# Quantising the next input tile in three steps of the chunk loop instead of two

## The chip, the cores and the metric

The kernel runs on one core of a Trainium2 chip. The metric is the device time of one execution in microseconds (us); the time before is 1630.95 us, the median of three runs. In the profile, PE is TensorE, PEld its weight loads, DVE is VectorE, ACT is ScalarE, POOL is GpSimd and SP is SyncE, whose queue starts the transfers.

## What is computed

A decoder layer with three blocks for 8 batches of 512 rows of 512 values. Only the last block is touched by the change. Its input and its inner result are rounded in blocks of 32 values with a common power of two as scale; the sum of the three parts is the output.

```
x = x + dilated_self_attention(layernorm(x))
x = x + cross_attention(layernorm(x), ctx_512, Wq, Wkv_expand, Wout)
x = x + ffn(layernorm(x), w_gate, w_up, w_down)

def ffn(x):                                   # weights quantised too
    inter = silu(q_act(x) @ w_gate.T) * (q_act(x) @ w_up.T)
    return q_act(inter) @ w_down.T

def q_act(x):                                 # blocks of 32 along the last axis
    sexp  = floor(log2(max|x| of the block)) - 2
    q     = round_to_small_float(x / 2**sexp) # 2 exponent, 3 mantissa bits, at most 7.5
    return q * 2**sexp
```

## The kernel before

Until about 178 us the weights of the last block are quantised and turned, and the self attention of batch 0 runs. Then each of the 8 batches goes through the same two stages. The first is cross attention (some 82 us, lines 871 to 886 and their counterparts on the other engines). The second is the chunk loop, which the change touches: `for i in range(P1_STEPS)`, with steps 0 to 20, of which 0 to 15 bring a chunk of the last block. Tile t of a batch (128 rows, four tiles) has the chunks 4t to 4t+3 (512 of the 2048 inner columns each). Beside these chunks run, in the same loop, the self attention and the head of the cross attention of the next batch; the last batch (b = 7) has none of that beside it.

Every engine has its own list, written out by hand in program order, and they meet through semaphores alone. What one step of the loop holds:

- TensorE: at i % 4 == 0 `turn_xq(t)` turns the quantised input tile `xq` into PSUM (line 1168) and `keep_busy` adds four products that nothing reads (L1060). Then `gate_up(i)` (L1181) makes gate and up of the chunk. It needs the slot that `gated(i - 2)` sets free, since the slots A and B alternate. Then come `down(i - 4)` (L1203) and `turn_inter(i - 3)` (L1192), and then the pieces of the next batch's attention: the turn L639, the scores L647, the value product L529 and the output L657, one after another over the four steps of a tile.
- ScalarE: `take_xq` copies the turned tile (L988), `silus(i)` (L995), `take_inter(i - 3)` (L1003), and for the next batch a copy, the exponential of the scores (L619, with a table load before it and one after it, ahead of the next silu) and a copy.
- VectorE: `gated(i)` multiplies up by silu (L838), takes block maxima (L812), their exponents (L815), the scales (L845) and their reciprocals (L846). `round_inter(i - 1)` clips and rounds into `q8` (L808). Then come `take_down` at steps 7, 11, 15 (L855), statistics (L498 to L500), and for the next batch the sums and divisions (L576, L578, L585), `normalise` (L511) and `shift2_of` (L516).
- GpSimd: `scale_inter(i)` and `scale_back(i - 1)` multiply by scales (both recorded at L696: `inter<-inter,rscale` and `iq<-q,scale`), `power` makes a reciprocal root (L506), `attend_pool` adds (L544), and `scale_x` and `scale_back_x` do for the next input tile what the first two do for a chunk (L696: `x_f<-x_f,rscale` and `xq<-q,scale`).

The next input tile t+1 is quantised during tile t. At step 4t, `quantise_x(t + 1)` on VectorE does normalisation into `x_f` (L511), maxima (L812), exponents (L815), scales (L827) and reciprocals (L828). GpSimd's `scale_x(t + 1)` stands at the end of step 4t. At step 4t+1, `round_x(t + 1)` on VectorE (L808, `q<-x_f`) is followed by GpSimd's `scale_back_x(t + 1)` at the end of the step. `turn_xq(t + 1)` on TensorE needs it at step 4t+4. For tile 0 this is done ahead of the loop.

Of the kernel before, what the change touches and what calls it, by code (L numbers as in the profile page):

```python
# [45 lines left out]
RING = 4  # L46
# [60 lines left out]
def decoder_layer(nc, x, ctx_t, wq_t, wkv_t, wo_t, w_gate, w_up, w_down, out):  # L107
# [3 lines left out]
    T = N // P  # L111
# [15 lines left out]
    with es:  # L127
# [92 lines left out]
        def until_filled(eng, label):  # L220
            s, k = slot_of[label]
            eng.wait_ge(filled[s], k + 1)
# [63 lines left out]
        with nc.Block() as block:  # L286
            @block.sync
            def _(sp):
                for j in range(RAW):
                    load_weights(sp, j)  # L290
                sp.dma_start(wq_raw[:], wq_t.rearrange("(c p) n -> p c n", p=P)).then_inc(wq_loaded, 16)
                sp.dma_start(wkv_raw[:], wkv_t).then_inc(wkv_loaded, 16)
                sp.dma_start(wo_sb[:], wo_t.rearrange("(c p) n -> p c n", p=P)).then_inc(wo_loaded, 16)
                for j in range(STEPS - RAW):

                    sp.wait_ge(wy_ready, j + 1)
                    load_weights(sp, j + RAW)
                sp.wait_ge(wo_loaded, 16)
# [204 lines left out]
        def power(pool, p, t):  # L503
            k = (p - 1) * T + t % T
            pool.wait_ge(S[f"var{p}_ready"], t + 1)
            pool.tensor_tensor(rstd[:, k:k + 1], var_eps[:, k:k + 1], minus_half[:],  # L506
                               ALU.pow).then_inc(S[f"rstd{p}_ready"], 1)

        def normalise(dve, dst, src, p, t):
            k = (p - 1) * T + t % T  # L510
            return dve.tensor_scalar(dst, src, moments[:, k, 0:1], rstd[:, k:k + 1], ALU.subtract, ALU.mult)  # L511
# [157 lines left out]
        with nc.Block() as block:  # L669
# [22 lines left out]
            @block.gpsimd  # L692
            def _(pool):

                def by_scales(dst, src, scales, signal):
                    pool.tensor_tensor(dst.rearrange("p (n k) -> p n k", k=BLOCK),  # L696
                                       src.rearrange("p (n k) -> p n k", k=BLOCK),
                                       scales.unsqueeze(2).to_broadcast([P, CH // BLOCK, BLOCK]),
                                       ALU.mult).then_inc(S[signal], 1)

                def scale_x(t):
                    pool.wait_ge(S["scale_x"], t + 1)
                    by_scales(x_f[:], x_f[:], rscale[:, RING, :], "x_scaled")

                def scale_back_x(t):
                    pool.wait_ge(S["q8x_ready"], t + 1)
                    if t >= 2:
                        until_filled(pool, ("xqT", t - 2))
                    by_scales(xq[:, t % 2, :], q8[:, RING + t % 2, :], scale6[:, RING + t % 2, :], "xq_ready")

                def scale_inter(i):
                    pool.wait_ge(S["scales_ready"], i + 1)
                    by_scales(inter[:, i % RING, :], inter[:, i % RING, :], rscale[:, i % RING, :],
                              "scaled_ready")

                def scale_back(i):
                    pool.wait_ge(S["q8_ready"], i + 1)
                    if i >= RING:
                        until_filled(pool, ("interT", i - RING))
                    by_scales(iq[:, i % RING, :], q8[:, i % RING, :], scale6[:, i % RING, :], "iq_ready")  # L720

                for i in range(P1_STEPS):
                    attend_pool(pool, 0, i)
                for b in range(B):
                    last = b + 1 == B
                    power(pool, 3, b * T)
                    scale_x(b * T)
                    power(pool, 3, b * T + 1)
                    scale_back_x(b * T)
                    if not last:  # L730
                        attend_pool(pool, b + 1, 0)
                    for i in range(P1_STEPS):
                        if i < CHUNKS:
                            scale_inter(b * CHUNKS + i)
                        if 1 <= i <= CHUNKS:
                            scale_back(b * CHUNKS + i - 1)
                        if i in STATS_AT:
                            power(pool, 3, b * T + STATS_AT[i])
                        if i and not last:
                            attend_pool(pool, b + 1, i)  # L740
                        if i % 4 == 0 and i // 4 + 1 < T:
                            scale_x(b * T + i // 4 + 1)
                        if i % 4 == 1 and i // 4 + 1 < T:
                            scale_back_x(b * T + i // 4 + 1)

            @block.vector
            def _(dve):
# [62 lines left out]
                def powers_of(src, r):  # L810

                    link(dve.tensor_reduce(top[:, r, :], in_blocks(src), AX_X, ALU.max,  # L812
                                           apply_absolute_value=True))
                    bits = top[:, r, :].bitcast(I32)
                    link(dve.tensor_scalar(bits, bits, EXPONENT, None, ALU.bitwise_and))  # L815

                def quantise_x(t):
                    r = RING + t % 2
                    dve.wait_ge(S["rstd3_ready"], t + 1)
                    if t:  # L820
                        dve.wait_ge(S["q8x_ready"], t)
                    link(normalise(dve, x_f[:], x_res[:, t % T, :], 3, t))
                    powers_of(x_f[:], RING)
                    if t >= 2:

                        dve.wait_ge(S["xq_ready"], t - 1)
                    link(dve.tensor_scalar(scale6[:, r, :], top[:, RING, :], TINY, ACT_SHIFT, ALU.max, ALU.mult))  # L827
                    dve.reciprocal(rscale[:, RING, :], scale6[:, r, :]).then_inc(S["scale_x"], 1)  # L828

                def round_x(t):  # L830
                    dve.wait_ge(S["x_scaled"], t + 1)
                    clip(q8[:, RING + t % 2, :], x_f[:]).then_inc(S["q8x_ready"], 1)
# [37 lines left out]
                for b in range(B):  # L870

                    first, end = b * UNITS, (b + 1) * UNITS
                    for pr in range(2):
                        maxima(first, pr)
                    for u in range(first, end):
                        oc, qt = units[u]
                        more = oc % OC + 1 < OC
                        if u + 1 < end:
                            maxima(u + 1, 0)
                        take_probs(u, 0)  # L880
                        recips(u)
                        if place[qt] == 0 and oc % OC:
                            take_out(oc - 1)
                        if u + 1 < end:
                            maxima(u + 1, 1)
                        take_probs(u, 1)
                    take_out((b + 1) * OC - 1)

                    last = b + 1 == B
                    take_y(b * T)  # L890
                    moments3(b * T)
                    take_y(b * T + 1)
                    quantise_x(b * T)
                    take_y(b * T + 2)
                    moments3(b * T + 1)
                    round_x(b * T)
                    if not last:
                        attend_vector(dve, link, b + 1, 0)
                    take_y(b * T + 3)
                    if not last:  # L900
                        attend_vector(dve, link, b + 1, 1)
                    for i in range(P1_STEPS):
                        if i < CHUNKS:
                            gated(b * CHUNKS + i)
                        if i % 4 == 3 and i > 4:
                            take_down(b * T + i // 4 - 1)
                        if 1 <= i <= CHUNKS:
                            round_inter(b * CHUNKS + i - 1)
                        if i in STATS_AT:
                            moments3(b * T + STATS_AT[i])  # L910
                        if i >= 2 and not last:
                            attend_vector(dve, link, b + 1, i)
                            head(b + 1, i)
                        if i % 4 == 0 and i // 4 + 1 < T:
                            quantise_x(b * T + i // 4 + 1)
                        if i % 4 == 1 and i // 4 + 1 < T:
                            round_x(b * T + i // 4 + 1)

            @block.scalar
# [378 lines left out]
```

## Time and profile before

| | us |
|---|---|
| median of 3 runs | 1630.95 (1624.5 to 1632.29) |
| profiled execution, its own time | 1628.43 |
| span of the profile | 1626.6 |
| busy: TensorE, VectorE, ScalarE, GpSimd | 1372.0, 1152.6, 859.4, 546.8 |
| chunk loop of batch 1, first gate product to last silu product | 468.8 to 537.7 |
| chunk loop of batch 7, first gate product to last addition | 1557.7 to 1623.3 |

The busy time over the whole span hides that the stages have different limits, so the rows below are taken from the chunk loops. Batch 1 stands for the batches 0 to 6: the 16 gate products (L838) of a chunk loop stand at the same distances from one another in all seven, within 0.1 us. In a timeline row, the first number is the start of the instruction, the second its duration. What is in brackets at the end is how long the engine stood idle before it and who ended that. The profile can show an instruction as started while it is still held back; its duration is then longer than that of its like.

### The profile page before, as it was taken

The page shows a single profiled execution, that of the slowest core. Times are in us where ns is not written, and L with a number is a line of the kernel's source. Part 1 is how long each engine was busy: PE and PEld are TensorE (multiplying, and loading weights), DVE is VectorE, ACT ScalarE, POOL GpSimd, SP SyncE. Part 2 cuts the span into 40 slices and gives each one's busy share as a digit, 9 for nine tenths or more (in the row PEclk, how much of TensorE's full clock was granted, in tenths as well). Part 3 has the DMA queues.
Part 4 walks back from the last instruction along what each step waited for, and adds up shares of the span by engine and source line. Part 5 has one row for each costly group of instructions (what it writes and reads, how often), then busy time and mean ns, then how long its engine had stood idle before and what let it go on. Part 6 is the DMA issues. An engine that isn't in the chain of part 4 may idle for free.

```text
span 1626.6 us, 31184 instructions
## 1 busy us (share of the span) xinstructions
PE 1372.0 (84%) x11267; PEld 792.3 (49%) x11344; DVE 1152.6 (71%) x2475; ACT 859.4 (53%) x2098; POOL 546.8 (34%) x494
## 2 busy tenths in 40 slices
PE   0223999889998899889998999889988899889987
PEld 0112665445544565445544564455544564455533
DVE  8995555885569656985679555985579556975577
ACT  2542564556635664556635564556635664556622
POOL 5883100660037201660047201660047201750055
PEclk9999999999999999999999999999999999999999
DMA  6321000000010000000010000000010000000001
GB/s 199 98 78 39 1 2 14 21 14 15 2 27 15 20 1 15 21 14 14 2 27 14 21 1 17 18 19 9 2 27 14 21 2 27 8 21 2 2 0 26
DMA packets 25285, 36.07 MB, mean 22 GB/s; under 512 B 2480, under 2 KB 10672, under 8 KB 25136
## 3 DMA queue, kind: packets, MB, share of 16 engines
q1 hardware_dynamic: 25136, 34.09, 7.8%
q8 instruction: 93, 1.52, 0.4%
q14 instruction: 56, 0.46, 0.1%
HBM read 25.69 MB, written 8.39 MB: 21 GB/s over the span
## 4 chain that ended last, share of the span: by engine, by line
PE 43%; DVE 32%; ACT 7%; issue 6%; POOL 3%; DMA 0%; SPq 0%; ACTq 0%; POOLq 0%; DVEq 0%
PE psum L1103 9%; PE psum L1120 9%; PE psum L529 8%; DVE top L812 6%; PE psum L1141 5%; DVE inter L838 4%; PE psum L1157 4%; DVE q L808 3%; PE psum L1106 3%; ACT p L957 3%; DVE nmx L762 2%; DVE top L815 2%; DVE stats L498 2%; DVE x_f L511 2%; DVE tmp L585 1%
## 5 line engine op out<-in xcount | busy, mean ns | idle before, releaser
L762 DVE TENSOR_REDUCE nmx<-psum 128x2 f32<-128x1024 f32 (+3 forms) x256 | 210.7, 823 | 167.0 <-PE psum L1106 166.3
L506 POOL TENSOR_TENSOR rstd<-var_eps,minus_half 128x1 f32<-128x1 f32 x96 | 58.2, 610 | 794.2 <-DVE var_eps L500 793.9
L957 ACT ACTIVATE p<-psum,nmx 128x384 f32<-128x384 f32 (+3 forms) x512 | 265.8, 527 | 64.0 <-DVE nmx L762 42.9
L775 DVE COPY pt<-psum 128x512 f32<-128x512 f32 (+3 forms) x256 | 124.7, 487 | 129.1 <-PE psum L1120 127.5
L1120 PE MATMUL psum<-ident,p 128*128 128x128 f32 x1280 | 204.8, 281 | 12.5 <-ACT pt L981 6.9
L1103 PE MATMUL psum<-k_f,q_f 32*128 32x512 f32 (+3 forms) x1024 | 206.9, 480 | 5.8 <-ACT p L957 5.3
L696 POOL TENSOR_TENSOR inter<-inter,rscale 128x512 f32<-128x512 f32 x128 | 140.1, 1095 | 143.7 <-DVE rscale L846 134.1
L1203 PE MATMUL psum<-wd_sb,iq_t 128*128 128x512 bf16 x483 | 135.3, 394 | 35.9 <-DVE x_res L855 29.3
L1120 PEld LDWEIGHTS psum<-ident,p 128*128 128x128 f32 x1280 | 138.6, 140 | 53.4 <-issue 19.0
L981 ACT COPY pt<-psum 128x512 f32<-128x512 f32 (+3 forms) x256 | 109.2, 426 | 97.8 <-PE psum L1120 95.5
L1181 PE MATMUL psum<-wg_sb,xq_t 128*128 128x512 bf16 x504 | 134.7, 391 | 20.3 <-DVE inter L838 20.3
L995 ACT ACTIVATE silu<-psum 128x512 f32<-128x512 f32 x128 | 76.4, 597 | 142.4 <-PE psum L1181 142.2
L696 POOL TENSOR_TENSOR iq<-q,scale 128x512 bf16<-128x512 fp8e4 x128 | 143.7, 1123 | 8.7 <-DVE q L808 8.7
L1003 ACT COPY iq_t<-psum 128x512 bf16<-128x512 bf16 x128 | 74.9, 585 | 123.9 <-PE psum L1192 123.9
L1181 PE MATMUL psum<-wu_sb,xq_t 128*128 128x512 bf16 x510 | 136.2, 391 | 0.1
L1157 PE MATMUL psum<-wo_sb,xn 128*128 128x512 f32 x256 | 118.0, 610 | 6.5 <-DVE xn L790 6.5
L428 PE MATMUL psum<-ident_b,w_q 128*128 128x128 bf16 x192 | 26.3, 309 | 112.7 <-POOL w_q L335 108.7
L1103 PEld LDWEIGHTS psum<-k_f,q_f 32*128 32x128 f32 x1024 | 76.9, 183 | 61.7 <-issue 43.2
L838 DVE TENSOR_TENSOR inter<-psum,silu 128x512 f32<-128x512 f32 x128 | 86.2, 674 | 24.6 <-ACT silu L995 23.9
L957 ACT ACTIVATION_READ_ACCUMULATOR p<-psum,nmx 128x1 f32 x512 | 103.0, 201 | 0.0
L529 PE MATMUL psum<-x_t,wq_hl 128*128 128x512 f32 (+1 forms) x480 | 100.1, 358 | 0.3
L1141 PE MATMUL psum<-pt,v_sb 128*32 128x128 f32 x2560 | 96.4, 277 | 3.2
(104 smaller groups left out, 2372.3 us busy)
## 6 DMA issues: line engine op xcount, KB each, us to landing
x_in<-in_x_dram SPq DMA_DIRECT2D x32, 256.0 KB, 4.0
out_dram<-x_res SPq DMA_DIRECT2D x64, 128.0 KB, 2.4
w_raw<-in_w_gate_dram SPq DMA_DIRECT2D x16, 256.0 KB, 2.8
w_raw<-in_w_up_dram SPq DMA_DIRECT2D x16, 256.0 KB, 3.1
w_raw<-in_w_down_dram SPq DMA_DIRECT2D x16, 256.0 KB, 3.9
ctx_in<-in_ctx_t_dram SPq DMA_DIRECT2D x8, 256.0 KB, 2.8
wq_raw<-in_wq_t_dram SPq DMA_DIRECT2D x1, 1024.0 KB, 8.4
wo_sb<-in_wo_t_dram SPq DMA_DIRECT2D x1, 1024.0 KB, 10.1
```

The lines of the kernel that those rows point to most:

```text
L529: last = pe.matmul(dst, w, x, start=(n == 0), stop=(stop and n == len(terms) - 1))
L696: pool.tensor_tensor(dst.rearrange("p (n k) -> p n k", k=BLOCK), src.rearrange("p (n k) -> p n k", k=BLOCK), scales.unsqueeze(2).to_broadc ...
L762: dve.tensor_reduce(nmx2[:, u % UNITS, 2 * pr:2 * pr + 2], where(("scores2", oc, qt, pr))[:, :, 0:(qt + 1) * P], AX_X, ALU.max, negate=Tru ...
L775: free(dve.tensor_copy(pt2[:, hh, 0:m], where(label)[:, 0, 0:m]), label)
L838: free(dve.tensor_tensor(inter[:, r, :], where(label)[:, 1, :], silu[:, i % 2, :], ALU.mult), label)
L957: ins = act.activation(p2[:, (4 * u + hh) % P2_RING, 0:m], where(label)[:, hh % 2, 0:m], ACT.Exp, bias=nmx2[:, u % UNITS, hh:hh + 1], accu ...
L1103: pe.matmul(where(label)[:, j, 0:m], q_f[rows, oc % 2, qt * P:(qt + 1) * P], k_f[rows, oc % 2, 0:m], start=True, stop=False)
L1120: last = pe.transpose(where(label)[:, 0, kt * P:(kt + 1) * P], p2[:, (4 * u + hh) % P2_RING, kt * P:(kt + 1) * P], ident[:])
L1141: last = pe.matmul(where(("outT", oc))[rows, 0, qt * P:(qt + 1) * P], v_sb[:, kt, h * HD:(h + 1) * HD], pt2[:, hh, kt * P:(kt + 1) * P], s ...
L1157: last = pe.matmul(where(label)[:, 0, :], out_n[:, oc, t % T * P:(t % T + 1) * P], wo_sb[:, oc, :], start=(oc == 0), stop=(oc == OC - 1))
L1181: last = pe.matmul(where(label)[:, j, :], xq_t[:, t % 2, c * P:(c + 1) * P], w[:, c, m * CH:(m + 1) * CH], start=(c == 0), stop=(c == C - 1))
L1203: last = pe.matmul(where(label)[:, 0, :], iq_t[:, i % RING, j * P:(j + 1) * P], wd_sb[:, 4 * m + j, :], start=(m == 0 and j == 0), stop=(m ...
```

## The change

`quantise_x` is split into `normalise3` and `scales_x`. Ahead of the loop the two are called one after the other, as before. In the loop, VectorE does `normalise3` at i % 4 == 0, `scales_x` at i % 4 == 1 (was 0) and `round_x` at i % 4 == 2 (was 1). GpSimd's `scale_x` stands at i % 4 == 1 (was 0) and `scale_back_x` at i % 4 == 2 (was 1), both at the end of the step. TensorE, ScalarE and SyncE keep their lists. No instruction is added or removed. In the changed kernel the lines behind `normalise3` have numbers two higher (L838 is L840 there), and those of TensorE's part five higher.

```diff
@@ GpSimd, chunk loop
-                        if i % 4 == 0 and i // 4 + 1 < T:
+                        if i % 4 == 1 and i // 4 + 1 < T:
                             scale_x(b * T + i // 4 + 1)
-                        if i % 4 == 1 and i // 4 + 1 < T:
+                        if i % 4 == 2 and i // 4 + 1 < T:
                             scale_back_x(b * T + i // 4 + 1)
@@ VectorE
-                def quantise_x(t):
-                    r = RING + t % 2
+                def normalise3(t):
                     dve.wait_ge(S["rstd3_ready"], t + 1)
                     if t:
                         dve.wait_ge(S["q8x_ready"], t)
                     link(normalise(dve, x_f[:], x_res[:, t % T, :], 3, t))
+
+                def scales_x(t):
+                    r = RING + t % 2
                     powers_of(x_f[:], RING)
...
@@ VectorE, chunk loop
                         if i % 4 == 0 and i // 4 + 1 < T:
-                            quantise_x(b * T + i // 4 + 1)
+                            normalise3(b * T + i // 4 + 1)
                         if i % 4 == 1 and i // 4 + 1 < T:
+                            scales_x(b * T + i // 4 + 1)
+                        if i % 4 == 2 and i // 4 + 1 < T:
                             round_x(b * T + i // 4 + 1)
```

VectorE's list from the end of step 4 to the start of step 6 of the first batch's chunk loop, before:

```order
347 L511 TENSOR_SCALAR x_f<-x_res,moments,rstd 128x512
348 L812 TENSOR_REDUCE top<-x_f 128x16
349 L815 TENSOR_SCALAR top<-top 128x16
350 L827 TENSOR_SCALAR scale<-top 128x16
351 L828 RECIPROCAL rscale<-scale 128x16
352 L838 TENSOR_TENSOR inter<-psum,silu 128x512
...
357 L808 TENSOR_SCALAR q<-inter 128x512
358 L516 SCALAR_TENSOR_TENSOR shift<-moments,rstd 128x1
359 L808 TENSOR_SCALAR q<-x_f 128x512
360 L838 TENSOR_TENSOR inter<-psum,silu 128x512
```

The same list in the changed kernel, up to the start of step 7:

```order
347 L511 TENSOR_SCALAR x_f<-x_res,moments,rstd 128x512
348 L840 TENSOR_TENSOR inter<-psum,silu 128x512
...
353 L808 TENSOR_SCALAR q<-inter 128x512
354 L516 SCALAR_TENSOR_TENSOR shift<-moments,rstd 128x1
355 L812 TENSOR_REDUCE top<-x_f 128x16
356 L815 TENSOR_SCALAR top<-top 128x16
357 L829 TENSOR_SCALAR scale<-top 128x16
358 L830 RECIPROCAL rscale<-scale 128x16
359 L840 TENSOR_TENSOR inter<-psum,silu 128x512
...
371 L808 TENSOR_SCALAR q<-x_f 128x512
372 L840 TENSOR_TENSOR inter<-psum,silu 128x512
```

The four scale instructions moved behind the rounding and the shift of step 5, and the rounding of `x_f` moved from ahead of step 6 to its end, behind two sets of statistics.

GpSimd's list for the steps 4 to 6 of the second tile, before:

```order
87 L506 TENSOR_TENSOR rstd<-var_eps,minus_half 128x1
88 L696 TENSOR_TENSOR x_f<-x_f,rscale 128x512
89 L696 TENSOR_TENSOR inter<-inter,rscale 128x512
90 L696 TENSOR_TENSOR iq<-q,scale 128x512
91 L696 TENSOR_TENSOR xq<-q,scale 128x512
92 L696 TENSOR_TENSOR inter<-inter,rscale 128x512
```

And in the changed kernel:

```order
86 L506 TENSOR_TENSOR rstd<-var_eps,minus_half 128x1
87 L696 TENSOR_TENSOR inter<-inter,rscale 128x512
88 L696 TENSOR_TENSOR iq<-q,scale 128x512
89 L696 TENSOR_TENSOR x_f<-x_f,rscale 128x512
90 L696 TENSOR_TENSOR inter<-inter,rscale 128x512
91 L696 TENSOR_TENSOR iq<-q,scale 128x512
92 L506 TENSOR_TENSOR rstd<-var_eps,minus_half 128x1
93 L696 TENSOR_TENSOR xq<-q,scale 128x512
```

Each of the two products for `x_f` and `xq` stands one step later, `xq` behind the powers of that step.

## Rows read from the trace of the kernel before

**Rows 1.** The windows view: loops of batches 1, 7; PE, PEld, DVE, ACT, POOL busy, PEclk.

```profile
468.80:540.40 71.60, 62.05 (x538) 33.42 (x546) 65.39 (x160) 39.98 (x60) 47.39 (x47) 0.97 0.07 16
1557.70:1615.80 58.10, 47.06 (x256) 22.04 (x261) 51.36 (x122) 20.11 (x33) 39.34 (x38) 1.00 0.05 10
```

**Rows 2.** Timeline of VectorE, batch 1, steps 4 to 8.

```profile
492.00 1.25 DVE L511 TENSOR_SCALAR x_f<-x_res,moments,rstd 128x512 f32<-128x512 f32 x1
...
494.60 0.63 DVE L838 TENSOR_TENSOR inter<-psum,silu 128x512 f32<-128x512 f32 x1
...
496.85 1.00 DVE L516 SCALAR_TENSOR_TENSOR shift<-moments,rstd 128x1 f32<-128x1 f32 x1
497.77 0.41 DVE L808 TENSOR_SCALAR q<-x_f 128x512 fp8e4<-128x512 f32 x1
498.11 0.68 DVE L838 TENSOR_TENSOR inter<-psum,silu 128x512 f32<-128x512 f32 x1
...
499.54 0.58 DVE L815 TENSOR_SCALAR top<-top 128x16 int32<-128x16 int32 x1
...
502.83 0.68 DVE L838 TENSOR_TENSOR inter<-psum,silu 128x512 f32<-128x512 f32 x1
...
504.26 0.17 DVE L815 TENSOR_SCALAR top<-top 128x16 int32<-128x16 int32 x1
...
508.55 0.69 DVE L838 TENSOR_TENSOR inter<-psum,silu 128x512 f32<-128x512 f32 x1
```

**Rows 3.** Timeline of GpSimd, batch 1, steps 5 and 6.

```profile
499.05 1.04 POOL L696 TENSOR_TENSOR xq<-q,scale 128x512 bf16<-128x512 fp8e4 x1
...
502.77 1.06 POOL L506 TENSOR_TENSOR rstd<-var_eps,minus_half 128x1 f32<-128x1 f32 x2
```

**Rows 4.** Timeline of TensorE, batch 1: a slow and a fast gate product, and turns.

```profile
495.29 1.88 PE L1181 MATMUL psum<-wg_sb,xq_t 128*128 128x512 bf16 x4 [0.88 <-DVE inter L838]
...
501.69 0.40 PE L1168 MATMUL psum<-ident_b,xq 128*128 128x128 bf16 x4
...
502.79 1.03 PE L1181 MATMUL psum<-wg_sb,xq_t 128*128 128x512 bf16 x4
...
524.50 1.02 PE L1203 MATMUL psum<-wd_sb,iq_t 128*128 128x512 bf16 x4 [0.28 <-DVE x_res L855]
...
531.87 0.38 PE L1192 MATMUL psum<-ident_b,iq 128*128 128x128 bf16 x4 [0.28 <-POOL iq L696]
```

**Rows 5.** Timeline of ScalarE, batch 1, silu of chunk 8.

```profile
504.71 0.60 ACT L995 ACTIVATE silu<-psum 128x512 f32<-128x512 f32 x1 [2.01 <-PE psum L1181]
```

**Rows 6.** Timeline of VectorE, batch 1, start of step 15.

```profile
536.97 0.69 DVE L838 TENSOR_TENSOR inter<-psum,silu 128x512 f32<-128x512 f32 x1 [0.61 <-ACT silu L995]
```

**Rows 7.** Timeline of VectorE, batch 7: first products of the four tiles.

```profile
1560.23 0.69 DVE L838 TENSOR_TENSOR inter<-psum,silu 128x512 f32<-128x512 f32 x1 [3.11 <-ACT silu L995]
...
1573.53 0.68 DVE L838 TENSOR_TENSOR inter<-psum,silu 128x512 f32<-128x512 f32 x1
...
1589.43 0.68 DVE L838 TENSOR_TENSOR inter<-psum,silu 128x512 f32<-128x512 f32 x1
...
1604.34 0.68 DVE L838 TENSOR_TENSOR inter<-psum,silu 128x512 f32<-128x512 f32 x1
```

**Rows 8.** Windows view, TensorE: around its waits of over 2 us.

```profile
536.30:539.70 3.40, 1.59 (x35) 1.00 0.00 0
539.70:543.10 3.40, 2.52 (x10) 0.50 0.37 80
...
1611.50:1615.00 3.50, 1.83 (x11) 1.00 0.00 0
1615.00:1618.40 3.40, 1.95 (x12) 1.00 0.36 77
```

**Rows 9.** Timeline of TensorE: the two waits that lie in Rows 8.

```profile
540.16 1.48 PE L1203 MATMUL psum<-wd_sb,iq_t 128*128 128x512 bf16 x3 [2.27 <-DVE x_res L855]
...
1615.77 1.02 PE L1203 MATMUL psum<-wd_sb,iq_t 128*128 128x512 bf16 x4 [2.39 <-DVE x_res L855]
```

More of the change, by code:

```diff
@@ L892, in _ @@
                     take_y(b * T + 1)
-                    quantise_x(b * T)
+                    normalise3(b * T)
+                    scales_x(b * T)
                     take_y(b * T + 2)
```

## The prediction

> **What bounds the kernel now.** The change touches only the chunk loops, so I read these first, by the windows view [rows 1]. With attention beside the chunks (batches 0 to 6), VectorE is busy for 65.39 of 71.60 us, TensorE for 62.05. In batch 7 it is 51.36 of 58.10 against 47.06. Next I read VectorE's timeline [rows 2]. From the normalisation at step 4 to the gate product of step 8 it has no idle time in brackets, so VectorE sets the pace. It doesn't run freely, though: the shift of 128x1 took 1.00 us, an exponent step of 128x16 took 0.58 us against 0.17 for a free one, and the normalisation of `x_f` took 1.25 us. Each of them overlaps a GpSimd product and ends with it. TensorE comes to the turn of `xq` at 501.69 [rows 4], long after GpSimd finished the product at 499.05 + 1.04 = 500.09 [rows 3]. So today nothing waits for `xq`. Its spare time is what the change spends. At the end of the loop this is different: the gate product of step 15 waits 0.61 us for silu [rows 6], so there the chain over TensorE and ScalarE sets the pace.
>
> **VectorE's own time: about zero.** I lay the changed list over batch 1, with durations of rows 2. The normalisation ends at 492.00 + 1.25 = 493.25, as before. The four scale instructions took 494.60 - 493.25 = 1.35 us and are gone from here, so the gate product of step 5 starts at 493.25. Gate, scales and rounding of a step take 496.85 - 494.60 = 2.25, which brings the shift to 495.5. It again meets GpSimd's product of the same chunk and again costs 497.77 - 496.85 = 0.92, to 496.4. Now the scales of `x_f` run: 1.35, plus up to 0.35 since the exponent step meets the end of the next GpSimd product. I take 1.6, to 498.0 (before: 498.11). Step 6 took 502.83 - 498.11 = 4.72 less the 0.41 by which the exponent step was held (0.58 against 0.17), since `xq` is no longer multiplied just then: 4.31, to 502.3. The rounding of `x_f` follows, 498.11 - 497.77 = 0.34. It meets the two powers of GpSimd, 1.06 us together [rows 3]. No row shows a rounding inside a power; the bounds are 0 and 0.4 us (the rest of the first one). Step 7 then starts between 502.7 and 503.1, against 502.83 before. The sum for VectorE alone is 0 +- 0.3 us per tile, and I take 0. The held time moves from one instruction to another; it doesn't go away.
>
> On this the Trainium skill has a rule (SBUF — State Buffer, "SBUF: two separate sides"): VectorE and GpSimd share a pair of ports under an exclusive lock, and the loser blocks for the other's whole instruction. The 0.92 of rows 2 agrees with it. By it a power holds the lock as a product does, so the upper bound of 0.4 would hold: some 0.4 us for each of two tiles in seven batches, at most 6 us.
>
> **What moves: `xq` comes 4.3 us later, and TensorE waits for it.** The rounding of `x_f` ends near 502.7. The powers stand ahead of the product on GpSimd and end near 503.4 (0.4 sooner than before, since VectorE passed step 6 faster). The product takes 1.04, to 504.4. TensorE came to the turn at 501.69, so it now waits some 2.8 us. Queued behind the turn on TensorE are the next tile's gate and up, then `down`, `turn_inter` and the next batch's scores. At full clock, the silu of the new tile starts 502.79 - 501.69 = 1.10 (turn, copy and the unused products) and 504.71 - 502.79 = 1.92 later [rows 4, 5], so at 507.6, and ends 0.60 later at 508.2. VectorE asks for it at 508.55 [rows 2]. The wait is hidden by 0.4 us. In the first tile the same walk leaves 0.1 us.
>
> **Full clock, batches 0 to 6: +1.7 us each.** The third tile has no such cover at its end. TensorE starts the tile 12 to 15 some 2.3 us late. Its list has only two idle spots of 0.28 us from there on [rows 4], so it arrives 1.7 us late at the scores of step 14, whose exponential (with its table loads) stands ahead of the silu of chunk 15 on ScalarE. VectorE already waits 0.61 us for that silu [rows 6], so all of it comes through: 7 x 1.7 = 11.9 us.
>
> **Full clock, batch 7: +5.5 us.** No attention lies beside the chunks, so steps are short and nothing covers the longer chain. From a tile's first gate product to the next tile's there are now: step 4 with 2.25 + 1.25; step 5 with 2.25 and scales of 1.35, or 2.15 when one of them is held by a whole product; step 6 with 2.25, one set of statistics (4.31 - 2.25 = 2.06 for two, so 1.03) and the rounding of 0.34, or 1.2 when held; then the product with 1.1 and its way over turn, copy, gate, up and silu, 1.10 + 1.92 + 0.60 + 0.2 = 3.8. The second tile takes 15.6 to 17.3 against 15.9 before, the third (no statistics) 14.6 to 16.3 against 14.9, the first (no first rounding, normalisation not held) 14.5 to 16.2 against 13.3 [rows 7]. The differences sum to 0.6 up to 5.7. I take 5.5, since in rows 2 an instruction was held wherever a product was under way.
>
> **The clock: +27 us.** TensorE's new waits are of a kind that the trace shows. In the chunk loops it waits over 2 us eight times, always for `down`. Around seven of them its clock goes to half (0.50, so 1.2 of 2.4 GHz), as at 539.70. Around one, at 1611.5 to 1618.4, it stays up [rows 8, 9]. The four gate matmuls of 495.29 took 1.88 us at half clock, those of 502.79 took 1.03 [rows 4], and up is the same again: 2 x 0.85 = 1.7 us more. At 539.70 the slow stretch began ahead of the wait's end and lasted 3.4, so most of the product after the new waits would fall in it. I take 1.45 us per fall. Less the covers of 0.1, 0.4 and 0 us, that leaves 1.25 on average for the 21 tile changes of batches 0 to 6, and 1.45 for the 3 of batch 7. Seven in eight of them fall: (21 x 1.25 + 3 x 1.45) x 7/8 = 26.8 us.
>
> The Trainium skill (TensorE: Matmul & The Clock Gate, "HAM oscillation — how this bites in real kernels") tells of half clock for waits between bursts that are longer than those here. Taken as it stands it would leave the clock up and give rival one. The seven falls of rows 8 speak against it.
>
> **Sum.** 0 + 11.9 + 5.5 + 26.8 = 44.2 us on the profiled execution's 1628.4: 1672.6. The median of the runs is 2.5 us above that execution, so I forecast 1675 us.
>
> **Rivals.**
> 1. The clock stays up at the new waits. Then only 17.4 us remain: 1648. For it: one of eight waits, and in the new waits TensorE comes from dense work. Chance 0.2.
> 2. Half of the waits bring the clock down, or the slow stretch ends before the product: 17.4 + 13.4, so 1662. Chance 0.2.
> 3. Faster. The spread takes `xq` off VectorE's way: in each of 21 tile changes the held exponent step (0.41) goes, and a held rounding of 0.9 in the first tile of each batch too, and the turn still comes before VectorE asks. That is 21 x 0.41 + 7 x 0.9 = 15 us, less 5.5 in batch 7: 1621. It decides if TensorE's lateness at step 14 is below the 0.6 us of slack it would need, against my 1.7. Chance 0.04.
> 4. No change that can be told: the first part of rival 3 and the lateness of 1.7 both come about, and batch 7 takes its lower bound. 1631 - 15 + 12 + 0.6, so 1629 to 1638. Chance 0.08. That the edit does nothing at all is excluded, since both lists do change.
>
> **How the numbers follow.** My forecast (falls at most waits) has a chance of 0.48. The range must reach the full-clock case and, above, the power bound of 6 us and 1.7 for every fall: 1643 to 1690. Within 0.5% (8 us) is about what a measurement of this kernel can tell from no change: slower than that are forecast and rivals 1 and 2, 0.88; within it 0.08; faster 0.04.
>
> **What would show it.** Right: TensorE's row of the turn (L1173 in the changed kernel) with 2 to 3 us idle ended by GpSimd's `xq`; `xq` ending some 4.3 us later after the step's gate product; more stretches at clock 0.50, one behind each tile change; the gate product of step 15 waiting about 2 us for silu; batch 7's loop over 5 us longer. Wrong: if the turn doesn't wait, the walk of step 6 is wrong; if it waits at clock 1.00, rival 1 holds; if VectorE's walk from 493.25 to 503 comes out over 1 us shorter, the held time did go away and rivals 3 or 4 hold.

## The result and the profile after

The changed kernel takes 1699.2 us (median of 4 runs, 1697.3 to 1700.0) against 1629.3 for the kernel before on the same occasions (median of 4; the 1630.95 above is that of three of them): a ratio of 1.0434, with a 95% interval of 1.0414 to 1.0454. It is slower by 70 us, where 44 us were forecast and the range ended at 1690.

| | before | after |
|---|---|---|
| profiled span, us | 1626.6 | 1698.2 |
| mean granted clock of TensorE | 0.983 | 0.952 |
| first gate product of batch 0 to that of batch 7, us | 287.78 to 1560.23: 1272.5 | 287.76 to 1612.92: 1325.2 |
| from there to the end, us | 66.4 | 85.3 |

So the 71.6 us of the profile are 52.7 in the batches 0 to 6 and 18.9 in batch 7. The clock row can be turned into a time: with only the two levels 1 and 0.5, a mean of 0.952 over 1698.2 us is 2 x 0.048 x 1698.2 = 163 us at half clock, against 2 x 0.017 x 1626.6 = 55 before.

VectorE's timeline of batch 1, steps 4 to 8 (it answers to [rows 2]; start, duration, idle time before in brackets):

```profile
500.22 1.26 DVE L511 TENSOR_SCALAR x_f<-x_res,moments,rstd 128x512 f32<-128x512 f32 x1
501.51 0.69 DVE L840 TENSOR_TENSOR inter<-psum,silu 128x512 f32<-128x512 f32 x1
...
503.83 1.00 DVE L516 SCALAR_TENSOR_TENSOR shift<-moments,rstd 128x1 f32<-128x1 f32 x1
504.75 0.67 DVE L812 TENSOR_REDUCE top<-x_f 128x16 f32<-128x512 f32 x1
505.46 0.39 DVE L815 TENSOR_SCALAR top<-top 128x16 int32<-128x16 int32 x1
...
506.26 0.63 DVE L840 TENSOR_TENSOR inter<-psum,silu 128x512 f32<-128x512 f32 x1
...
510.52 0.42 DVE L808 TENSOR_SCALAR q<-x_f 128x512 fp8e4<-128x512 f32 x1
510.85 0.68 DVE L840 TENSOR_TENSOR inter<-psum,silu 128x512 f32<-128x512 f32 x1
...
517.62 0.69 DVE L840 TENSOR_TENSOR inter<-psum,silu 128x512 f32<-128x512 f32 x1 [0.97 <-ACT silu L1000]
```

From the normalisation to step 7's gate product VectorE needs 510.85 - 500.22 = 10.63 us, against 502.83 - 492.00 = 10.83 before [rows 2]. The walk of the prediction had 0 +- 0.3. The held time only moved: the shift is still held (1.00), the exponent step of `x_f` now is (0.39 against 0.17), and that of step 6 no longer (0.17 at 507.64, where it was 0.58). What is new is the bracket in the last row: VectorE waits for the silu of the new tile.

GpSimd and TensorE, batch 1, the same tile change (it answers to [rows 3, 4]):

```profile
510.46 1.06 POOL L506 TENSOR_TENSOR rstd<-var_eps,minus_half 128x1 f32<-128x1 f32 x2
511.49 1.04 POOL L696 TENSOR_TENSOR xq<-q,scale 128x512 bf16<-128x512 fp8e4 x1
```

```profile
507.88 1.12 PE L657 MATMUL psum<-xn,e 64*64 64x32 f32 x32
512.68 0.58 PE L1173 MATMUL psum<-ident_b,xq 128*128 128x128 bf16 x4 [3.68 <-POOL xq L696]
513.49 1.48 PE L1065 MATMUL psum<-wd_sb,ident_b 128*128 128x512 bf16 x3 [0.22 <-issue]
514.77 1.32 PE L1186 MATMUL psum<-wg_sb,xq_t 128*128 128x512 bf16 x4
```

TensorE stands 3.68 us ahead of the turn, waiting for `xq`. Over all 24 tile changes it is 3.2 to 4.0 us in the batches 0 to 6, and 5.8, 5.4 and 4.9 us in batch 7. After this wait everything runs slowly at first: the turn takes 0.58 us (0.40 before), and from its start to the gate product it is 514.77 - 512.68 = 2.09 us, where it was 1.10. So it is at 17 of the 24 changes. At the other seven the clock falls only after the turn has started, and the two rows are 1.08 to 1.90 us apart, as here in batch 4, where the gate product is slow and the turn isn't:

```profile
1101.31 0.38 PE L1173 MATMUL psum<-ident_b,xq 128*128 128x128 bf16 x4 [3.17 <-POOL xq L696]
...
1102.39 1.85 PE L1186 MATMUL psum<-wg_sb,xq_t 128*128 128x512 bf16 x4
```

Batch 7, VectorE at its three tile changes (it answers to [rows 7]), and TensorE at the first:

```profile
1632.38 0.69 DVE L840 TENSOR_TENSOR inter<-psum,silu 128x512 f32<-128x512 f32 x1 [5.57 <-ACT silu L1000]
...
1652.89 0.69 DVE L840 TENSOR_TENSOR inter<-psum,silu 128x512 f32<-128x512 f32 x1 [4.41 <-ACT silu L1000]
...
1672.98 0.69 DVE L840 TENSOR_TENSOR inter<-psum,silu 128x512 f32<-128x512 f32 x1 [4.58 <-ACT silu L1000]
```

```profile
1626.07 0.58 PE L1173 MATMUL psum<-ident_b,xq 128*128 128x128 bf16 x4 [5.79 <-POOL xq L696]
1626.88 1.49 PE L1065 MATMUL psum<-wd_sb,ident_b 128*128 128x512 bf16 x3 [0.22 <-issue]
1628.16 1.91 PE L1186 MATMUL psum<-wg_sb,xq_t 128*128 128x512 bf16 x4
1629.87 1.85 PE L1186 MATMUL psum<-wu_sb,xq_t 128*128 128x512 bf16 x4
1631.55 1.03 PE L1208 MATMUL psum<-wd_sb,iq_t 128*128 128x512 bf16 x4
```

VectorE was never idle at these places before. The windows view of TensorE around two of the waits (busy time, then clock; it answers to [rows 8]):

```profile
508.60:512.00 3.40, 0.41 (x14) 0.99 0.00 0
512.00:515.40 3.40, 2.50 (x9) 0.51 0.17 36
1621.20:1624.60 3.40, 0.00 (x0) 1.00 0.00 0
1624.70:1631.50 6.80, 5.21 (x15) 0.50 0.01 2
```

Behind both waits the clock is at half, the second time for 6.8 us at a stretch, so that the turn, the unused products, gate and up all fall in it. The clock's record has such a stretch at each of the 24 changes, of 3.4 us at 15 of them and of 6.8 us at 9.

### The profile page after: what moved, and what is told of

Read it like the earlier page. It is cut to its first block, busy times and chain, and to the rows that moved or that the text cites. A ratio compares the mean times of both kernels' runs of the same rounds, so it can differ in the third digit from the quotient of the medians.

```text
span 1698.2 us, 31208 instructions
## 1 busy us (share of the span) xinstructions
PE 1401.5 (83%) x11267; PEld 813.5 (48%) x11344; DVE 1156.3 (68%) x2475; ACT 857.8 (51%) x2098; POOL 543.8 (32%) x494
## 4 chain that ended last, share of the span: by engine, by line
PE 52%; DVE 18%; POOL 8%; issue 7%; ACT 7%; DMA 0%; SPq 0%; ACTq 0%; POOLq 0%; DVEq 0%
PE psum L1108 9%; PE psum L1125 8%; PE psum L529 7%; PE psum L1186 7%; PE psum L1146 4%; PE psum L1162 4%; DVE top L812 3%; PE psum L1208 3%; PE psum L1065 3%; PE psum L1111 3%; ACT p L962 3%; DVE inter L840 2%; DVE nmx L762 2%; POOL xq L696 2%; POOL x_f L696 2%
## 5 line engine op out<-in xcount | busy, mean ns | idle before, releaser
L1186 PE MATMUL psum<-wg_sb,xq_t 128*128 128x512 bf16 x504 | 147.4, 419 | 1.7 <-issue 1.1
L840 DVE TENSOR_TENSOR inter<-psum,silu 128x512 f32<-128x512 f32 x128 | 86.6, 677 | 85.6 <-ACT silu L1000 84.7
L1186 PE MATMUL psum<-wu_sb,xq_t 128*128 128x512 bf16 x510 | 141.9, 403 | 0.3 <-issue 0.2
L696 POOL TENSOR_TENSOR iq<-q,scale 128x512 bf16<-128x512 fp8e4 x128 | 138.7, 1084 | 8.7 <-DVE q L808 8.7
L993 ACT COPY xq_t<-psum 128x512 bf16<-128x512 bf16 x32 | 18.8, 587 | 198.1 <-PE psum L1173 198.1
```

Of the source, the lines that this page charges most:

```text
L840: free(dve.tensor_tensor(inter[:, r, :], where(label)[:, 1, :], silu[:, i % 2, :], ALU.mult), label)
L1186: last = pe.matmul(where(label)[:, j, :], xq_t[:, t % 2, c * P:(c + 1) * P], w[:, c, m * CH:(m + 1) * CH], start=(c == 0), stop=(c == C - 1))
```

## The experiments

Theory A: `xq` comes late, TensorE waits, and this costs twice, once by the longer chain and once by the clock that falls in the wait. Rival B: the chain is nearly all of it. Rival C: VectorE's new order costs. Idea D, the prediction's third rival: what GpSimd holds of VectorE could be won back. (The text put on record for that run calls this its theory A, and the opposite rival D.) Ratios are against the kernel before in the same rounds, with 95% intervals.

**The clock kept up.** The changed kernel, and in `turn_xq`:

```diff
                     until_free(pe, label)
+                    if t % T:
+                        keep_busy(label, 14)
                     pe.wait_ge(S["xq_ready"], t + 1)
```

> The changed kernel, with 14 unused products of TensorE (3.0 us at full clock) put ahead of each wait for xq inside the chunk loop (24 places), so that TensorE is not idle there. Theory A (the late xq costs about 20 us through the longer chain, and the rest, about 50 us, is the half clock that TensorE's idle time brings): the stretches at half clock go back to about the 15 of before, and the time is 1645 to 1655. Rival B (the longer chain is nearly all of it, the half clock only shows it): 1690 or more, since the chain is the same.

Measured: 1649.7 us, ratio 1.0155 (1.0124 to 1.0185), clock 0.983 as before the change. TensorE in batch 1:

```profile
497.83 3.19 PE L1065 MATMUL psum<-wd_sb,ident_b 128*128 128x512 bf16 x13
501.50 0.40 PE L1175 MATMUL psum<-ident_b,xq 128*128 128x128 bf16 x4 [0.48 <-POOL xq L696]
501.74 1.03 PE L1065 MATMUL psum<-wd_sb,ident_b 128*128 128x512 bf16 x4
502.60 1.03 PE L1188 MATMUL psum<-wg_sb,xq_t 128*128 128x512 bf16 x4
```

`xq` is as late as in the changed kernel (the turn starts 15.7 us after the gate product of step 4, there 15.8), but the turn takes 0.40 again and the gate product comes 1.10 after it. Work that nobody reads brought back 49 us of the profiled span. Theory A, and B is out. This run also gives the price of the longer chain. Batch 0 to batch 7 takes 283.40 to 1572.18, so 1288.8 us, 16.3 more than before. Of these, 7 x 1.5 = 10.4 lie in the loops. The other 5.9 lie behind them, nearly all in the batches 4, 5 and 6 (1.8 to 2.0 each), where this run has 6.8 us at half clock behind the wait at step 16 and the kernel before 3.4, so I count it to the clock. The loop of batch 7, from its first to its last gate product, takes 60.2, 7.5 more.

In batch 7 the clock fell only behind the wait at the very end, and it shows the level in one column of equal work:

```profile
1635.21 1.02 PE L1210 MATMUL psum<-wd_sb,iq_t 128*128 128x512 bf16 x3 [2.39 <-DVE x_res L857]
1636.07 0.39 PE L1199 MATMUL psum<-ident_b,iq 128*128 128x128 bf16 x4
1637.14 1.89 PE L1210 MATMUL psum<-wd_sb,iq_t 128*128 128x512 bf16 x4 [0.68 <-ACT iq_t L1008]
```

Before the change the same wait of 2.39 us was the one of eight behind which the clock stayed up [rows 9]. Here the clock falls behind it, and the time from the last gate product to the end is 3.0 us longer (16.7 against 13.6), with the same work. The length of the wait alone doesn't decide it.

**Half of the filling.** The same with `keep_busy(label, 7)`.

> The changed kernel with half as many unused products ahead of the turn, 7 in 24 places (1.5 us), which leaves TensorE idle 1.8 to 2.5 us there in batches 0 to 6 and over 3 us in batch 7. Theory A: the clock follows the idle time that is left. If 2 us of idle are enough to bring it down, as at seven of eight waits before, the time is 1675 to 1700; if not, in batches 0 to 6 it stays up and only batch 7 pays: 1655 to 1665. Rival B (longer chain, not clock) is out by the run with 14.

Measured: 1670.2 us, ratio 1.0261 (1.0231 to 1.0290), clock 0.970, so 100 us at half. TensorE waits 1.6 to 2.3 us in the batches 0 to 6. This lies between the two ranges, 5 us from either: 12 of these 21 waits bring the clock down. Again it isn't their length that decides, since five of 1.97 us never did and six of 2.06 or 2.07 us always. Laid side by side, the spans of the run with 14 products, of this one and of the changed kernel are 1649, 1674 and 1698 us with 56, 100 and 163 us at half clock: 0.57 and 0.38 us of time per us at half clock.

**Only `xq` late.** The kernel before, GpSimd alone:

```diff
-                        if i % 4 == 1 and i // 4 + 1 < T:
+                        if i % 4 == 2 and i // 4 + 1 < T:
                             scale_back_x(b * T + i // 4 + 1)
```

> The kernel before, with GpSimd's product for xq alone moved one step later (i % 4 == 2); VectorE's order is that of before. Theory A (what costs is that xq comes late): as the changed kernel within 8 us, 1690 to 1705, with TensorE waiting over 3 us for xq at each tile change. Rival C (VectorE's new order costs, by what it holds and what it delays): 1629, as before.

Measured: 1692.5 us, ratio 1.0419 (1.0387 to 1.0451). VectorE's order is that of before, and nearly the whole loss is there. TensorE waits 2.7 to 3.2 us for `xq` in batches 0 to 6, a little less than the "over 3" expected. At 21 of the 24 changes the clock falls. The three where it stays up are waits of 3.16 us, while it fell behind all seven of 2.65. TensorE in batch 4, with the clock of the windows behind the two waits:

```profile
1056.92 0.38 PE L1168 MATMUL psum<-ident_b,xq 128*128 128x128 bf16 x4 [3.16 <-POOL xq L696]
...
1098.22 0.38 PE L1168 MATMUL psum<-ident_b,xq 128*128 128x128 bf16 x4 [2.65 <-POOL xq L696]
```

```profile
1056.90:1060.30 3.40, 3.33 (x18) 1.00 0.02 5
1099.20:1102.60 3.40, 3.40 (x10) 0.52 0.36 77
```

**The same with the clock kept up**, by `keep_busy(label, 12)` as above.

> GpSimd's product for xq one step later, VectorE's order of before, and 12 unused products (2.6 us) ahead of the turn, so that the clock stays up. Theory A (late xq plus clock is all of it): the slow stretches go back to about 15 to 18, and the time is 1640 to 1655, as the changed kernel with 14 unused products (1650), since VectorE's new order by itself costs nothing. Rival C (part of the change's full-clock cost is VectorE's new order): 1630 to 1638.

Measured: 1654.6 us, ratio 1.0138 (1.0115 to 1.0161), clock 0.986. This agrees with 1.0155 for the changed kernel with filling, within the intervals. So rival C has nothing left in either part that would exceed these intervals, some 0.3%.

**The same spread, one step sooner.** The changed kernel with

```diff
-                        if i % 4 == 0 and i // 4 + 1 < T:
-                            normalise3(b * T + i // 4 + 1)
-                        if i % 4 == 1 and i // 4 + 1 < T:
+                        if i % 4 == 3 and i // 4 + 2 < T:
+                            normalise3(b * T + i // 4 + 2)
+                        if i % 4 == 0 and i // 4 + 1 < T:
                             scales_x(b * T + i // 4 + 1)
-                        if i % 4 == 2 and i // 4 + 1 < T:
+                        if i % 4 == 1 and i // 4 + 1 < T:
                             round_x(b * T + i // 4 + 1)
```

GpSimd's two products at steps 0 and 1, and the first `normalise3` ahead of the loop.

> The three parts spread over three steps as in the change, but each one step sooner: normalisation at i % 4 == 3 of the tile before, scales at 0, rounding at 1, GpSimd's products where they were before the change. Theory A: the same spread without a late xq; within 6 us of before, 1623 to 1635, no wait of TensorE for xq inside the loop. Rival C: VectorE's order is spread as in the change, so 1650 or more.

Measured: 1640.1 us, ratio 1.0098 (1.0068 to 1.0128). The clock is up (0.986), and TensorE doesn't wait for `xq` in batches 0 to 6. Yet it is 5 us above the top of the range expected, and part of the reason is on VectorE:

```profile
487.59 1.59 DVE L511 TENSOR_SCALAR x_f<-x_res,moments,rstd 128x512 f32<-128x512 f32 x1
489.21 0.69 DVE L840 TENSOR_TENSOR inter<-psum,silu 128x512 f32<-128x512 f32 x1
...
498.89 0.59 DVE L815 TENSOR_SCALAR top<-top 128x16 int32<-128x16 int32 x1
```

At its new place the normalisation meets GpSimd's addition (L544) and is held longer, 1.59 us against 1.25 at the old one [rows 2]. The exponent step of step 6 is held as before. And the gate product of step 4, which followed the divisions directly, now stands behind the normalisation: in batch 1 it came 6.95 us after that of step 3, against 5.32 before. The next one follows sooner (4.75 against 5.92), so that this spot costs 0.5 us. The loops of batches 0 to 6 are 0.7 to 1.0 us longer, 5.9 in all. The other 5 us up to batch 7 lie behind the loops, where this run's stretches at half clock lie otherwise than before; which of them cost it was not tested. I had counted VectorE's order as free wherever `xq` was in time. It was free in the change, where what was held anew was released elsewhere, but not here.

**Rounding first.** The changed kernel with `round_x` ahead of the statistics of its step and `scale_back_x` ahead of its powers:

```diff
+                        if i % 4 == 2 and i // 4 + 1 < T:
+                            round_x(b * T + i // 4 + 1)
                         if i in STATS_AT:
                             moments3(b * T + STATS_AT[i])
...
+                        if i % 4 == 2 and i // 4 + 1 < T:
+                            scale_back_x(b * T + i // 4 + 1)
                         if i in STATS_AT:
                             power(pool, 3, b * T + STATS_AT[i])
```

> The changed kernel, with the rounding of x_f ahead of the statistics of its step on VectorE, and GpSimd's product for xq ahead of that step's powers. xq comes 2 to 3 us sooner. Theory A: TensorE's waits shrink from 3.3 to 4 us to about 1 us and mostly no longer bring the clock down in batches 0 to 6; 1640 to 1665. Rival B: gains only what the chain gets shorter where VectorE waits, under 20 us: 1680 or more.

Measured: 1682.1 us, ratio 1.0360 (1.0324 to 1.0397), clock 0.957. Less was won than expected, and the time lies in the range of rival B. It doesn't speak for B, though: the run was to shrink TensorE's waits to about 1 us, and it didn't. VectorE and GpSimd at step 6 of batch 1:

```profile
501.45 1.26 DVE L808 TENSOR_SCALAR q<-x_f 128x512 fp8e4<-128x512 f32 x1
```

```profile
501.34 1.10 POOL L696 TENSOR_TENSOR inter<-inter,rscale 128x512 f32<-128x512 f32 x1 [0.93 <-DVE rscale L848]
502.40 1.22 POOL L696 TENSOR_TENSOR iq<-q,scale 128x512 bf16<-128x512 fp8e4 x1
503.58 1.04 POOL L696 TENSOR_TENSOR xq<-q,scale 128x512 bf16<-128x512 fp8e4 x1
504.59 1.06 POOL L506 TENSOR_TENSOR rstd<-var_eps,minus_half 128x1 f32<-128x1 f32 x2
```

On GpSimd only the two powers (1.06 us) stood between, and the product still queues behind the two products of the chunk. `xq` came 1 us sooner, not 2 to 3. The rounding now meets a product and takes 1.26 us instead of 0.42. TensorE's waits stayed at 2.7 us and more, and the clock still fell at 20 of the 24 changes.

**Batch 7 alone.** Changed order on VectorE and GpSimd if `last`, the old one otherwise.

> The changed order in batch 7 alone, that of before in the batches 0 to 6. The changed kernel's trace has its last 84.6 us where before has 65.7. If the batches don't act on one another: +19 us against before, 1644 to 1650. If part of it came from where batch 7 began: between +10 and +15.

Measured: 1645.5 us, ratio 1.0100 (1.0069 to 1.0131), so +16 us by the ratio, +18 by the medians. From the first gate product of batch 7 (1557.11) to the end (1640.9) it is 83.8 us, against 66.4 before and 85.3 in the changed kernel. So in the profiles the batches do not act on one another by more than 2 us. The ratio alone (+11 to +21 us) would leave both cases open.

**Held time, taken away at one place.** The kernel before, with

```diff
-            dve.scalar_tensor_tensor(out=shift2[:, t % T:t % T + 1], in0=moments[:, k, 0:1], scalar=-1.0,
-                                     in1=rstd[:, k:k + 1], op0=ALU.mult, op1=ALU.mult).then_inc(S["shift2_ready"], 1)
+            dve.tensor_scalar(shift2[:, t % T:t % T + 1], moments[:, k, 0:1], rstd[:, k:k + 1], -1.0,
+                              ALU.mult, ALU.mult).then_inc(S["shift2_ready"], 1)
```

> The kernel before, with the shift of 128x1 (L516) written as a product of one tensor with a scalar per partition instead of two tensors in SBUF. In the trace of before the two-tensor form is held 0.84 us by a GpSimd product in 21 places, while the statistics' scalar form of the same size (L500, 0.15 us) is never held. Theory A (VectorE sets the pace in steps 4 to 11, and held time there counts in full): the 14 holds of the first and second kind go and the time falls by 8 to 15 us, to about 1615. Rival D (held time isn't on the path, or the next instruction is held instead): within 4 us of before.

Measured: 1627.3 us, ratio 0.9996 (0.9977 to 1.0014). Taking the held time away gains nothing that can be told apart from zero, and at most 0.23% (4 us), where idea D had 8 to 15. VectorE in batch 1, step 5, in this run:

```profile
494.02 0.20 DVE L516 TENSOR_SCALAR shift<-moments,rstd 128x1 f32<-128x1 f32 x1
494.14 1.15 DVE L808 TENSOR_SCALAR q<-x_f 128x512 fp8e4<-128x512 f32 x1
```

The shift is free, 0.20 instead of 1.00. The rounding behind it is held instead, 1.15 instead of 0.41 [rows 2], and the gate product comes where it came. What frees both is the end of the same GpSimd product.

**Half clock at the end of the loop.** With that scalar shift, and then without it, 9 unused products ahead of TensorE's wait at step 16:

```diff
+                        if i == CHUNKS:
+                            keep_busy(("interT", b * CHUNKS + i - INTER_LAG), 9)
                         if INTER_LAG < i <= CHUNKS + INTER_LAG:
                             down(b * CHUNKS + i - INTER_LAG - 1)
```

> The previous kernel with the scalar shift, with 9 unused products on TensorE ahead of its wait of 2.3 us at step 16. Theory A: the half clock behind that wait goes in the batches where it stood (seven stretches of 3.4 us), and with it about 1 us each: 3 to 7 us under the scalar shift alone. Rival: the work in that stretch isn't on the path, no change.

> The kernel before with 9 unused products ahead of TensorE's wait at step 16, and nothing else. With the scalar shift beside it, the same edit brought half clock from 55 to 6.5 us and the time down by 0.3% at most. Theory A (half clock costs only where TensorE is waited for, and at step 16 and around it, it is not): half clock under 20 us, time within 6 us of before. Rival: half clock costs about half of its length wherever it stands, as in the changed kernel: 20 us or more faster.

Measured: 1622.3 us, ratio 0.9967 (0.9947 to 0.9988), clock 0.999; and 1622.1 us, ratio 0.9944 (0.9928 to 0.9961), clock 0.995. The first is 5 us below the scalar shift alone (1627.3), inside the 3 to 7 of theory A. The second is 8 us below the kernel before (9 by the ratio), outside the 6 us of theory A and far from the 20 of its rival. The time at half clock fell from 55 us to under 5 and to 16. So it did cost something, but little.

The profiles show where. In the kernel before, the batches 1, 2, 4, 5 and 6 have two stretches of 3.4 us at half clock each, and from first gate product to first gate product they take 180.9 to 181.2 us. The same five batches of the run with scalar shift and filling have none and take 180.9 to 181.2 too, each within 0.1 us of its like. These 34 us at half clock, behind step 4 and behind the wait at step 16, cost nothing. But batches 0 and 3 of the kernel before take 183.6 and 183.8 us. They alone have a stretch under the output products of the cross attention, where TensorE has 26 products to do in a row. TensorE in batch 0, and the same products in batch 1:

```profile
454.47 13.06 PE L1157 MATMUL psum<-wo_sb,xn 128*128 128x512 f32 x26 [0.81 <-DVE xn L790]
...
637.25 11.43 PE L1157 MATMUL psum<-wo_sb,xn 128*128 128x512 f32 x26 [0.81 <-DVE xn L790]
```

```profile
454.20:457.60 3.40, 3.13 (x4) 0.53 0.00 0
637.20:640.60 3.40, 3.35 (x8) 1.00 0.00 0
```

The stretch of 3.4 us costs 1.6 there, half its length. The other 1 us of these two batches comes between the loop and the output products; in both, the stretch at half clock behind step 16 lies later or is longer than in the others. In these two runs with filling, one of the 14 batches 0 to 6 has a slow start of the output products (182.8 us). Only one execution of each kernel was profiled, so that the rest of the 8 us isn't shown.

## Why the prediction was wrong in size

The direction and the mechanism came out, the sum did not: +44 us forecast, +70 measured (71.6 on the profiled spans). Term by term, on the profiled spans:

| term | forecast | measured | from |
|---|---|---|---|
| VectorE's own order | 0 | within the noise | last two filled runs agree |
| full clock, batches 0 to 6 | 11.9 | 10.4 | loops of the filled run against before |
| full clock, batch 7 | 5.5 | 7.5 | loop of the filled run against before |
| clock | 26.8 | 53.7 | rest: 71.6 - 17.9 |

- **VectorE's walk** held to 0.2 us. The place where I left both bounds open, a rounding inside a power, is settled too: at 510.52 the rounding starts within the powers of 510.46, takes 0.42 and isn't held, and the powers take their usual 1.06. So it is at all 14 such places. In the third tile the rounding starts 0.05 us behind the start of a product instead, at 530.24, and is held, 1.27 us. The rule of the Trainium skill (SBUF — State Buffer, "SBUF: two separate sides"), by which the instruction that starts first keeps the pair for its whole length, a GpSimd one of any kind included, is met by the products of this case but not by the 128x1 powers.
- **`xq` 4.3 us later.** Counted from the gate product of step 4, GpSimd ended it at 500.09 - 488.68 = 11.4 before and at 512.53 - 496.89 = 15.6 after: 4.2.
- **TensorE's wait** was 3.68, not 2.8 us. I had left TensorE's arrival where it was. But step 5's gate product now comes 1.3 us sooner and frees its slot sooner, and TensorE no longer has the slow stretch of 495.29 [rows 4]. It arrived 12.1 us after the gate product of step 4, against 13.0.
- **Full clock, batches 0 to 6.** With the clock kept up, the gate product of step 15 waits 1.76 us for silu in batch 1 (0.61 before), and comes 1.5 us later in the batch. That is the third tile's lateness, forecast as 1.7.
- **The clock, the step that failed.** I saw that the clock would fall, and 24 of 24 changes did it, where I had 7 in 8. But the term was 26.8 us and measured 53.7. Two things were left out of it. First, I priced a fall by the gate and up product alone, at 1.7 us, and rounded that down, with the turn and the unused products at full clock. They run at half clock as well: from the turn to the gate product it is up to 2.09 us instead of 1.10, and over the 24 changes 19 us more. At the first change of batch 7 the gate and up product adds 3.39 - 1.73 = 1.66, since the slow stretch lasted 6.8 us there. Second, no term had the half clock behind the loops, and there are 5.9 us of it behind the wait at step 16 (above, in the filled run) and 3.0 behind the last wait. 26.8 + 19 + 5.9 + 3.0 = 54.7, so that the rest is small. In that rest, falls at 24 changes instead of 21 and a longer wait stand against stretches that end before gate and up are done, and it is partly luck that they balance.
- **Rival 1** (the clock stays up) is refuted at each place. It had rested on one wait of eight. The Trainium skill's account (TensorE: Matmul & The Clock Gate, "HAM oscillation — how this bites in real kernels"), read as I had read it, would have led to 1648, and the trace of the changed kernel shows half clock behind all of its waits, from 3.16 us on, and that of the run with 7 products behind waits of 2.06 us. Rival 2, half of the falls, is out for the same reason: it was 24 of 24.
- **Rival 3** (held time goes away) fails on the scalar shift: the time held at one instruction is held at the next.
- **The range** ended at 1690 as it took 1.7 as the most that a fall can cost, and had nothing for the clock behind the loops. A bound should have been all that TensorE has to do between the wait and the product that VectorE asks for: (1.10 + 1.73) at double length, so 2.8 us, times 24.

## What to carry to other kernels

When an operand is made later, first ask who stands in line for it, and whether that engine is one whose clock depends on being busy. Then price the fall of the clock by everything that this engine does between the end of its wait and the result that is asked for, not by the large products alone. Half clock on an engine that is ahead costs nothing (34 us of it in five batches, no change within 0.1 us a batch), and about half its length on one that is waited for (1.6 of 3.4 us under the output products). Which of the two it is shows at the place, not in the mean clock. Filling such a wait with unused products tells the two parts apart in one run.

Time for which VectorE was held by GpSimd's products was not won here by making the held instruction cheaper, nor by spreading the work: the next one was held to the same end. Follow the end of the product, not the length of the row.

## What the runs showed that I had not expected

- A wait of 2.4 us is followed by half clock in one run and not in another with the same work at the same place (the last wait of batch 7, 1.03 against 1.89 us for four products of `down`). In the changed kernel it fell behind all 24 waits of 3.16 us and more, but with only GpSimd's product late it stayed up behind three of 3.16 us and fell behind seven of 2.65. In the kernel before it also fell six times behind two waits of 0.93 and 0.88 us, as at the slow gate product of 495.29 [rows 4]. So the length of the wait alone doesn't settle it; what does stays open.
- A two-operand 128x1 instruction of VectorE is held by a GpSimd product for up to 0.84 us, its scalar form (0.20 us) isn't. A reciprocal root of 128x1 on GpSimd, 0.53 us long, did not hold a rounding of 128x512 at any of 14 places, while one that started just inside a GpSimd product was held (1.26 or 1.27 us).
